# Down projection of a gated FFN: from full-precision matmuls to three fp32r passes with a VectorE-made rest

## What is computed

```
x = x + tanh(g_xattn) * attention(layernorm(x), ctx, ctx)     # Wq Wk Wv Wo, softmax over 77
n = layernorm(x)
gate = fp4_linear(n, w_gate)          # [rows, 256] x [256, 704]
y    = fp4_linear(n, w_up)
h    = silu(gate) * y                 # [rows, 704]
x    = x + tanh(g_ffn) * fp4_linear(h, w_down)     # [rows, 704] x [704, 256]
# fp4_linear(x, w): x and w each scaled by max|block of 16| / 6, rounded to
# {0, .5, 1, 1.5, 2, 3, 4, 6} with sign, scaled back, then x @ w.T
```

## Time and profile before

| | |
|---|---|
| runs | 322.92 us median, 321.5 to 323.33 |
| profiled execution | span 322.5 us from the first to the last instruction; the files give no separate time for this execution, the median lies 0.4 us above its span |
| busy | TensorE 286.2 us (89%), VectorE 260.5 (81%), ScalarE 160.1 (50%), GpSimd 131.8 (41%) |
| TensorE's granted clock | mean 0.959 of full speed, 1.00 from 100 to 256 us |
| L1123, `down` | 192 records (two per matmul), 50.5 us busy |

### The profile page before, as it was taken

The page is one execution under the profiler, slowest core; times in us unless marked ns, Lnnn a source line. Parts: engine busy times, 40 slices in busy tenths (PEclk is TensorE's granted clock), DMA queues, the critical chain, the costliest instruction groups (busy, mean ns, idle before and its releaser), DMA issues.

```text
span 322.5 us, 5666 instructions
## 1 busy us (share of the span) xinstructions
PE 286.2 (89%) x1634; PEld 243.7 (76%) x1634; DVE 260.5 (81%) x761; ACT 160.1 (50%) x514; POOL 131.8 (41%) x161
## 2 busy tenths in 40 slices
PE   3779797597899999999999999999999999978574
PEld 2459796486788888888888888888888988766452
DVE  1997788969679888888888888888898978867584
ACT  1136474456256565655656565565655555531111
POOL 0596253313515454545353544444444243442400
PEclk9999997989599999999999999999999999979598
DMA  5990000000000000000000000000000000000000
GB/s 117 346 306 2 1 1 0 2 0 0 0 4 16 5 14 18 1 16 0 16 0 16 0 16 0 16 0 16 0 19 0 17 2 16 0 18 0 17 0 33
DMA packets 9048, 8.50 MB, mean 26 GB/s; under 512 B 1580, under 2 KB 8775, under 8 KB 9031
## 3 DMA queue, kind: packets, MB, share of 16 engines
q1 hardware_dynamic: 7255, 7.50, 7.4%
q10 hardware_dynamic: 1776, 0.79, 0.9%
HBM read 6.19 MB, written 2.10 MB: 26 GB/s over the span
## 4 chain that ended last, share of the span: by engine, by line
PE 48%; DVE 25%; issue 14%; POOL 8%; ACT 2%; DMA 2%; SPq 1%; POOLq 0%; DVEq 0%; ACTq 0%
PE psT L1139 9%; PE psO L1123 9%; PE psG L1023 6%; PE psG L1024 5%; PE psG L1025 5%; DVE xc L745 3%; PE psO L1132 3%; PE psG L1053 3%; PE psO L1114 2%; PE psS L1023 2%; DVE xa L749 2%; POOL ha L993 2%; PE psS L1025 2%; DMA X<-in_x 2%; PE psS L1024 2%
## 5 line engine op out<-in xcount | busy, mean ns | idle before, releaser
L403 ACT ACTIVATE probs<-psS,negmax 128x77 f32<-128x77 f32 x256 | 62.0, 330 | 15.7 <-DVE negmax L609 15.7
L1123 PE MATMUL psO<-wdT,hT 128*128 128x256 f32 x192 | 50.5, 396 | 1.2 <-ACT hT L503 1.2
L1123 PEld LDWEIGHTS psO<-wdT,hT 128*128 128x128 f32 x192 | 32.5, 189 | 14.5 <-issue 5.3
L1023 PE MATMUL psG<-wgh,xqh 128*128 128x512 f32 (+1 forms) x96 | 42.3, 440 | 1.3 <-DVE xql L811 1.3
L993 POOL TENSOR_TENSOR ha<-hc,ha 128x704 f32<-128x704 bf16 x15 | 24.3, 1622 | 45.2 <-DVE ha L658 45.2
L1114 PE MATMUL psO<-vblk,pT 128*128 128x51 f32 x320 | 40.1, 274 | 1.2 <-ACT pT L424 1.2
L1114 PEld LDWEIGHTS psO<-vblk,pT 128*128 128x128 f32 x320 | 39.5, 197 | 1.7 <-ACT pT L424 1.7
L1024 PE MATMUL psG<-wgl,xqh 128*128 128x512 f32 (+1 forms) x96 | 37.7, 393 | 0.0
L1025 PE MATMUL psG<-wgh,xql 128*128 128x512 f32 (+1 forms) x96 | 37.7, 393 | 0.0
L617 DVE SCALAR_TENSOR_TENSOR tg<-th,psG 128x256 f32<-128x256 f32 (+1 forms) x48 | 19.1, 398 | 20.8 <-ACT th L409 20.5
L609 DVE TENSOR_REDUCE negmax<-psS 128x4 f32<-128x308 f32 x64 | 30.1, 470 | 5.7 <-PE psS L1025 5.7
(11 more groups left out here) (119 smaller groups left out, 668.6 us busy)
## 6 DMA issues: line engine op xcount, KB each, us to landing
out_x<-X SPq DMA_DIRECT2D x16, 128.0 KB, 1.7
X<-in_x SPq DMA_DIRECT2D x2, 512.0 KB, 9.8
wraw<-in_L_ffn_w_down SPq DMA_DIRECT2D x1, 704.0 KB, 9.2
wraw<-in_L_ffn_w_gate ACTq DMA_DIRECT2D x1, 640.0 KB, 9.6
wraw<-in_L_ffn_w_up SPq DMA_DIRECT2D x1, 640.0 KB, 7.7
X<-in_x SPq DMA_DIRECT2D x4, 128.0 KB, 6.3
X<-in_x SPq DMA_DIRECT2D x2, 256.0 KB, 9.2
vblk<-in_vmask SPq DMA_DIRECT2D x2, 255.0 KB, 7.3
```

The lines of the kernel that those rows point to most:

```text
L403: ins = act.activation(probs[:, p, hd * S:(hd + 1) * S], psS[g % 2][:, k * S:(k + 1) * S], ACT.Exp, bias=negmax[:, p, hd:hd + 1])
L1023: pe.matmul(o, ah, bh, start=first, stop=False)
L1123: return pe.matmul(psO[1][:, 0:D], hT[0:m, p, c * P:(c + 1) * P], wdT[0:m, c, :], start=(c == first), stop=(c == last))
```

## The change

`down` calls `mm3` on `hTh`/`hTl` and `wdh`/`wdl`. ScalarE's copies now write the rounded part (fp32r) and signal VectorE, which subtracts it from the bank and writes the rest; only then is TensorE released. Chunk 5 is padded to 128 rows with zeros. The weights are treated alike.

```diff
-        wdT = sb("wdT", [P, HC, D])
+        wdh = sb("wdh", [P, HC, D], F32R)
+        wdl = sb("wdl", [P, HC, D], F32R)
-        hT = sb("hT", [P, 2, HC * P])
+        hTh = sb("hTh", [P, 2, HC * P], F32R)
+        hTl = sb("hTl", [P, 2, HC * P], F32R)
...
# ScalarE
-                ins = act.activation(wdT[:, 2 * t:2 * t + full, :].rearrange("p c n -> p (c n)"),
+                ins = act.activation(wdh[:, 2 * t:2 * t + full, :].rearrange("p c n -> p (c n)"),
                                      psG[t % 2][:, 0:full * D], ACT.Copy)
...
-                ins.then_inc(w_ds, 1)
+                ins.then_inc(w_dh, 1)
...
-                    act.activation(hT[:, pd, 4 * P:], psT[1][:, 0:2 * P], ACT.Copy).then_inc(d_hTs, 1)
+                    act.activation(hTh[:, pd, 4 * P:], psT[1][:, 0:2 * P], ACT.Copy).then_inc(d_hTh, 1)
...
-                    act.activation(hT[:, pd, 0:4 * P], psT[0][:, :], ACT.Copy).then_inc(d_hTs, 1)
+                    act.activation(hTh[:, pd, 0:4 * P], psT[0][:, :], ACT.Copy).then_inc(d_hTh, 1)
...
-                        act.activation(hT[:, pd, a:a + m], psT[k][:, 0:m], ACT.Copy).then_inc(z_hTs, 1)
+                        act.activation(hTh[:, pd, a:a + m], psT[k][:, 0:m], ACT.Copy).then_inc(z_hTh, 1)
# VectorE
+            dve.memset(wdh[I % P:, HC - 1, :].bitcast(F32), 0.0).then_inc(s_fill, 1)
+            dve.memset(wdl[I % P:, HC - 1, :].bitcast(F32), 0.0).then_inc(s_fill, 1)
...
+            def weights_down_lo(t):
+                dve.wait_ge(w_dh, t + 1)
+                full = min(2, I // P - 2 * t)
+                ins = dve.tensor_tensor(wdl[:, 2 * t:2 * t + full, :].rearrange("p c n -> p (c n)"),
+                                        psG[t % 2][:, 0:full * D],
+                                        wdh[:, 2 * t:2 * t + full, :].rearrange("p c n -> p (c n)").bitcast(F32),
+                                        ALU.subtract)
+                if full < 2:
+                    ins = dve.tensor_tensor(wdl[0:I % P, 2 * t + 1, :], psG[t % 2][0:I % P, D:2 * D],
+                                            wdh[0:I % P, 2 * t + 1, :].bitcast(F32), ALU.subtract)
+                ins.then_inc(w_ds, 1)
+
+            def hidden_lo(n, p, k):
+
+                done(dve, d_hTh, 2, n, k + 1)
+                if k == 0:
+                    done(dve, d_dn, 1, n - 2)
+                a, m = (4 * P, 2 * P) if k == 0 else (0, 4 * P)
+                dve.tensor_tensor(hTl[:, p, a:a + m], psT[1 - k][:, 0:m], hTh[:, p, a:a + m].bitcast(F32),
+                                  ALU.subtract).then_inc(d_hTs, 1)
+
+            def last_lo(k, p):
+
+                chunks = PARTS[k][2]
+                a, m = chunks[0] * P, len(chunks) * P
+                dve.wait_ge(z_hTh, k + 1)
+                dve.tensor_tensor(hTl[:, p, a:a + m], psT[k][:, 0:m], hTh[:, p, a:a + m].bitcast(F32),
+                                  ALU.subtract).then_inc(z_hTs, 1)
...
                 if live(i - 3) and not just(i - 3, LAST):
                     h_bits(i - 3, pd)
+                if just(i, 2):
+                    for t in range(HC // 2):
+                        weights_down_lo(t)
...
                 if just(i - 2, LAST):
                     last_part(0, pc)
+                if live(i - 3) and not just(i - 3, LAST):
+                    hidden_lo(i - 3, pd, 0)
                 if live(i - 2):
                     gated(i - 2, pc, 2)
                 if live(i - 1):
                     x_max(i - 1)
                 if live(i - 2):
                     hidden(i - 2, pc, 2)
+                if live(i - 3) and not just(i - 3, LAST):
+                    hidden_lo(i - 3, pd, 1)
                 if just(i - 2, LAST):
+                    last_lo(0, pc)
                     residual_out(LAST - 1)
                     last_part(1, pc)
+                    last_lo(1, pc)
# TensorE
             def down(p, c, first, last):
 
-                m = min(P, I - c * P)
-                return pe.matmul(psO[1][:, 0:D], hT[0:m, p, c * P:(c + 1) * P], wdT[0:m, c, :], start=(c == first),
-                                 stop=(c == last))
+                at = slice(c * P, (c + 1) * P)
+                return mm3(psO[1][:, 0:D], hTh[:, p, at], hTl[:, p, at], wdh[:, c, :], wdl[:, c, :], c == first,
+                           c == last)
```

More of the change, by code:

```diff
@@ L202, in build @@
                                     "s_kl", "s_v", "s_vs", "s_vr", "s_vb", "s_tg", "s_gbo")]
-        (w_max, w_scale, w_inv, w_a, w_c, w_cb, w_t, w_r, w_q, w_T, w_hi, w_lo, w_dT, w_ds) = [
+        (w_max, w_scale, w_inv, w_a, w_c, w_cb, w_t, w_r, w_q, w_T, w_hi, w_lo, w_dT, w_dh, w_ds) = [
             sem(n) for n in ("w_max", "w_scale", "w_inv", "w_a", "w_c", "w_cb", "w_t", "w_r", "w_q", "w_T", "w_hi",
-                             "w_lo", "w_dT", "w_ds")]
+                             "w_lo", "w_dT", "w_dh", "w_ds")]
         (q_st, q_mv, q_ve, q_rstd, q_xn, q_xg, q_xnT, q_xnTs, q_q, q_hi, q_lo) = [
@@ L216, in build @@
                              "b_cb", "b_t", "b_r", "b_q")]
-        z_step, z_q, z_hT, z_hTs = [sem(n) for n in ("z_step", "z_q", "z_hT", "z_hTs")]
+        z_step, z_q, z_hT, z_hTh, z_hTs = [sem(n) for n in ("z_step", "z_q", "z_hT", "z_hTh", "z_hTs")]
         c_xT, c_hi, c_lo, c_gu, c_th, c_t1, c_h = [sem(n) for n in ("c_xT", "c_hi", "c_lo", "c_gu", "c_th", "c_t1", "c_h")]
-        (d_max, d_scale, d_inv, d_hr, d_a, d_c, d_cb, d_t, d_r, d_q, d_hT, d_hTs, d_dn, d_out, d_st) = [
-            sem(n) for n in ("d_max", "d_scale", "d_inv", "d_hr", "d_a", "d_c", "d_cb", "d_t", "d_r", "d_q", "d_hT", "d_hTs",
+        (d_max, d_scale, d_inv, d_hr, d_a, d_c, d_cb, d_t, d_r, d_q, d_hT, d_hTh, d_hTs, d_dn, d_out, d_st) = [
+            sem(n) for n in ("d_max", "d_scale", "d_inv", "d_hr", "d_a", "d_c", "d_cb", "d_t", "d_r", "d_q", "d_hT", "d_hTh", "d_hTs",
                              "d_dn", "d_out", "d_st")]
@@ L390, in weights_down @@
                 full = min(2, I // P - 2 * t)
-                ins = act.activation(wdT[:, 2 * t:2 * t + full, :].rearrange("p c n -> p (c n)"),
+                ins = act.activation(wdh[:, 2 * t:2 * t + full, :].rearrange("p c n -> p (c n)"),
                                      psG[t % 2][:, 0:full * D], ACT.Copy)
                 if full < 2:
-                    ins = act.activation(wdT[0:I % P, 2 * t + 1, :], psG[t % 2][0:I % P, D:2 * D], ACT.Copy)
-                ins.then_inc(w_ds, 1)
+                    ins = act.activation(wdh[0:I % P, 2 * t + 1, :], psG[t % 2][0:I % P, D:2 * D], ACT.Copy)
+                ins.then_inc(w_dh, 1)
             def exps(n, p, g):
@@ L1170, in iteration @@
                     pe.wait_ge(l_bv, 16)
-                    pe.wait_ge(s_fill, 3)
+                    pe.wait_ge(s_fill, 5)
                     for b in range(B):
```

## The result

The change makes the kernel slower: 353.81 us median (352.29 to 355.19, 4 runs) against 323.12 us (4 runs of the kernel before on the same chip), ratio 1.095, 95% interval 1.090 to 1.101. The profiled execution has a span of 353.3 us against 322.5. That execution took 355.19 us, and one of the kernel before with a span of 322.6 us took 324.47: 1.9 us lie around the span in both, so 30.8 us of span answer to 30.7 us of median. VectorE's lines stand 33 lower than before (L717 is L750, L662 is L695, L745 is L778), those of GpSimd and TensorE 42 (L1006 is L1048, L1114 is L1156).

What follows compares the result with a forecast made beforehand. A chain through TensorE and VectorE, with the down projection wholly on it, was taken as the bound. 13.2 + 1.5 + 1.0 + 0.6 + 1.65 + 5.5 = 23.5 us gave 346.4 median, with one clock fall 348; range 339 to 361.

Steps and rivals of the forecast that it cites:

- A pass costs 0.118 us: Down projection on TensorE: each of 18 fp32r passes takes 0.118 us at 256 columns, 2.1 us instead of 2.98.
- +1.5 us per tile by TensorE's waits, less 0.33: Steady loop: TensorE waiting for VectorE's subtractions adds 1.5 us per tile, sooner xq returns up to 0.33, net +1.2.
- so the mask waits less: VectorE's bit mask, held by GpSimd's L1006, would be held less, bringing xq up to 0.33 us sooner after the scores.
- the sum over 11 tiles, 13.2: Steady loop: 11 tiles at 1.2 us more each add 13.2 us.
- The down projection is wholly on the chain: Steady tile on TensorE: all 2.98 us of the down projection bound the kernel, and everything behind waits for it.
- The 13.6 us named as what the fewer passes could give: Down projections: 0.85 us of TensorE time saved per tile, 13.6 us over 16 tiles if all reached the end.
- The waits as the sole cause: Steady loop: TensorE standing still for the two subtractions ends the down projection 1.5 us later per tile.
- Rival B: Steady loop: waits are absorbed, TensorE runs at its own pace of 15.63 - 0.85, kernel ends at 317 us; chance 0.04.
- Weights, 1.65: Weight preparation, once: TensorE's third pair of transposes waits for VectorE's first weight subtraction; scores start 1.65 us later.
- The next three tiles, 3.1: Three down projections after the 11 steady tiles: 1.5, 1.0 and 0.6 us more.
- Tail, 5.5: Last tiles: subtractions stand behind the last tile's first quantization part; 4.7 us plus some half clock, taken as 5.5.
- Rival A: Whole loop: clock swings in a third or more of the tiles, 5 to 13 falls, 353 to 368 us; chance 0.25.

Runs made afterwards that it cites:

- Kernel A: The kernel before with only chunk 5 padded to 128 rows, still full-precision matmuls: 322.64 us, ratio 1.000.
- Kernel E: The kernel before plus VectorE's two subtractions per tile, written to a buffer nobody reads: 337.30 us (2 of 4 runs), 1.044 of the kernel before.
- Kernel D: The change with the third pass reading hTh, so TensorE never waits for the rest; VectorE's work unchanged: 352.66 us, 1.088 of the kernel before.
- kernel B: The change with VectorE's two hidden subtractions moved ahead of and behind x1_norm: 337.94 us, 1.045 of the kernel before.
- H: The change with subtractions early, passes reading the rest last, and x_c and mask ahead of GpSimd's step: 352.24 us, 1.091 of the kernel before.
- K: The change with subtractions early, rest passes last, and all of x's quantization ahead of GpSimd's step: 351.40 us, 1.087 of the kernel before.
- C: The change with TensorE's 12 passes on hTh first and the 6 on hTl last: 342.48 us, 1.060 of the kernel before.
- I: The kernel before with chunk 5 padded and x_c and mask moved ahead of GpSimd's step: 327.23 us, 1.006 of the kernel before.

## Why the prediction came out as it did

348 was forecast, 353.8 measured, inside the range. The time came out for reasons that were in part others than those forecast. By its own steps:

**A pass costs 0.118 us: right.** 199.84 to 202.83 has passes 0.12 apart. At half the clock they are 0.21 apart.

**+1.5 us per tile by TensorE's waits, less 0.33: right in size.** From x1_norm to the transposes of xn it was 2.35 us (186.71 to 189.06) and is 3.79: +1.44. From there to the transposes of xq it was 4.47 and is 4.39: only 0.08 given back. The step that failed is "so the mask waits less": GpSimd's L1048 comes 0.8 us later and now falls upon `x_c`, which is held in the mask's place, and TensorE could use only the 0.2 us that it had waited for xq. The forecast of 1.3 and 0.8 us for the two waits came out as 1.2 and 0.5; the sum over 11 tiles, 13.2, as 13.65. That is nearer than the steps deserve: a steady tile grew by 1.3 us and not 1.2, the first of the 11 did not grow at all (17.57 before, 17.46 after), and one fall of the clock put in some 1.25 us.

**"The down projection is wholly on the chain": half true.** Kernel A shows that shortening it by 0.3 us gains nothing. The 13.6 us named as what the fewer passes could give were never to be had: VectorE's path stood 0.2 us behind. I read the chain, which shows one of two paths that end nearly together, and it doesn't say how far behind the other is. The wait that does is the 0.20 us of TensorE for xq in the kernel before. And what I took for a detail, the mask that ends with GpSimd's L1006, is the place where the second path runs: that xq keeps its distance of 2.2 us from the end of that step is what the prediction left out.

**The waits as the sole cause: wrong as a reason, right as a sum, by luck.** Kernel E gives 0.75 us of the 1.3 with no wait for a rest, through the later reciprocal and GpSimd's later step; the waits account for the other 0.57 and not for 1.5. Kernel D, without one, is as slow as the change. Rival B's condition (the waits absorbed, 317 us) could not be met while VectorE carries 1.0 us more per tile.

**Weights, 1.65: too small, 3.9.** The chain of waits was right (third pair at 67.0, forecast 66.85; the scores at 69.6, forecast 69.25). Left out was that TensorE was then at half the clock until 74.5, through the scores and the first gate and up matmuls. The windows of the change and then of the kernel before over these matmuls:

```profile
68.00:72.00 4.00, 4.00 (x16) 3.62 (x15) 1.99 (x6) 1.75 (x7) 0.00 (x0) 0.50 0.00 0
```
```profile
68.00:70.00 2.00, 2.00 (x12) 1.66 (x11) 0.80 (x3) 0.36 (x3) 0.00 (x0) 1.00 0.00 0
```

The clock was already at half at 57.4, ahead of the first new wait there; why is not settled, but it cost nothing: kernel B, which differs from the change only behind this place, had the full clock from 56 to 64 us and needed 22.97 us from x1_norm of iteration 1 to that of iteration 2, the change 23.00. In both the clock stayed at half until 74.5, where before it was back at 67.6.

**The next three tiles, 3.1: too small, 6.7.** They hold three falls of the clock where the kernel before has one, and I had put one costly fall into the whole kernel (1.6 us). Two falls more at some 1.3 us are 2.6 of the missing 3.6; the rest was not traced.

**Tail, 5.5: it was 6.5.** TensorE stood still for 5.1 us where about 4 was forecast, and the passes behind it ran at half the clock.

**Rival A, a clock that swings in a third of the tiles**, did not come in the change (1 of 11) but in kernels D, H and K. The page "TensorE: Matmul & The Clock Gate" of the Trainium skill, section "A second HAM failure mode: psum-queue depth-cycling", has short pauses make the clock swing. The rows agree in part: stops of 0.6 to 1.3 us beside the 51-column matmuls were followed by a fall in 7 of ten tiles in D, 8 in H, 4 in K and 3 in E, and stops of 1.2 and 0.5 us around the 256-column passes in the change, and of 0.3 to 0.5 us in the 51-column stretch in A, B and C, went without falls in nearly every tile.

## What to carry to other kernels

When the chain of waits names one engine, look at what that engine itself waits for at the point where two paths meet: a wait of 0.2 us there says that all shortening beyond 0.2 is lost. Then follow the other path to its start, across engines: an instruction that ends with another engine's step in every tile belongs to that engine's path, though no wait is shown for it. Splitting an operand to save passes on TensorE costs VectorE two subtractions per tile here, and it pays only where they do not put off an instruction that releases such a path; here they did, and removing TensorE's waits took off only 0.55 us of 1.3. A stop among the 51-column matmuls was followed by a fall of the clock far more often than one around the 256-column passes; whether the width decides it was not tested by itself.

## What was not expected of the hardware

- **The hold is of a kind of instruction and ends 0.1 to 0.3 us after GpSimd's.** Three different VectorE steps were held beside the same GpSimd step: the mask (1.32 us instead of 0.23), `x_c` (1.02 instead of 0.28), `x_add` (1.18 instead of 0.41). Not held are the maxima, which read PSUM, and instructions that start after it. The page "SBUF — State Buffer" of the Trainium skill, section "Who interferes with whom", names two kinds that need the shared port pair: those in a 2-port mode and those with two SBUF inputs beside a GpSimd step that reads SBUF. `x_add` has two SBUF inputs, and I's rows agree.
- **A 64-row chunk among 128-row ones costs 0.3 us per down projection**, 3.15 against 2.84 us for the same 12 records; with the chunk padded with zeros the 0.3 us are gone.
- **The clock falls beside the 51-column matmuls** behind a stop of about 1 us: seven times in some ten tiles in kernel D, eight in H, three in E, nearly always for 3.4 us. A tile with one is some 1.3 us longer (17.7 against 16.4 us).
